# A causal attention block with a ternary feed-forward on one core: how the value products read and write their columns, and how the first score tile is formed

## The reference, cut to what matters

```python
# x: (2, 1024, 256) float32; 16 heads of 128
x = x + attention(layernorm(x), W_Q, W_K, W_V, W_O)
x = x + ffn(layernorm(x))                 # ternary weight, scale and shift, bias
...
q = einsum('bsd,hed->bhse', x, W_Q)       # k and v likewise
scores = where(causal, -1e9, einsum('bhse,bhme->bhsm', q, k) / sqrt(128))
z = einsum('bhsm,bhme->bhse', softmax(scores), v)
out = einsum('bhse,hde->bsd', z, W_O)
```

## Time and profile before

| | |
|---|---|
| time, median of 3 runs | 820.55 us (819.53 to 821.32) |
| the profiled execution | 819.02 us, of which the span of the instructions is 816.9 us |
| busy: PE, DVE, ACT, POOL | 808.9, 655.7, 558.7, 547.2 us |
| granted TensorE clock, mean | 1.000 |

### The profile page before, as it was taken

How to read it: one execution, slowest core, us unless ns; L and a number is a source line. 1 busy time by engine, 2 the same in 40 slices (tenths; PEclk the granted TensorE clock), 3 DMA queues, 4 the chain that set the end, 5 groups by cost and what they waited for, 6 DMA issues and landing times.

```text
span 816.9 us, 14674 instructions
## 1 busy us (share of the span) xinstructions
PE 808.9 (99%) x4878; PEld 726.5 (89%) x4878; DVE 655.7 (80%) x1438; ACT 558.7 (68%) x1031; POOL 547.2 (67%) x280
## 2 busy tenths in 40 slices
PE   8999999999999999999999999999999999999998
PEld 7988998888999888998888899888899888899887
DVE  7988787878777878778877878877878787878888
ACT  6877666667676666676766766666766766776684
POOL 6178765686666856768557785569675686585486
PEclk9999999999999999999999999999999999999999
DMA  6456656556556565566654676555766555555603
GB/s 187 95 140 144 171 136 142 117 135 166 138 134 151 134 153 123 139 146 149 161 122 112 152 177 143 127 119 126 175 140 141 130 130 141 128 138 137 150 6 105
DMA packets 57226, 111.50 MB, mean 136 GB/s; under 512 B 16960, under 2 KB 21184, under 8 KB 57152
## 3 DMA queue, kind: packets, MB, share of 16 engines
q1 hardware_dynamic: 57152, 110.56, 56.6%
HBM read 10.88 MB, written 2.10 MB: 16 GB/s over the span
## 4 chain that ended last, share of the span: by engine, by line
PE 95%; DVE 2%; SPq 1%; ACT 1%; DMA 0%; issue 0%; POOL 0%; POOLq 0%; ACTq 0%
PE ring L650 25%; PE scores L688 25%; PE ring L627 21%; PE ring L636 11%; PE ring L659 11%; SPq L445 1%; PE ring L668 1%; PE scores L750 1%; PE ring L591 1%; DMA pT<-turn 0%; DVE acc L861 0%; DVE turn L849 0%; PE ring L601 0%; DVE scores L841 0%; DVE stats L879 0%
## 5 line engine op out<-in xcount | busy, mean ns | idle before, releaser
L521 POOL TENSOR_TENSOR pT<-pT 128x1024 fp32r<-128x1024 f32 x186 | 444.4, 2407 | 256.9 <-ACT pT L786 256.3
L841 DVE CUSTOM_DVE_ANT_0 scores<-scores,mask 128x128 f32<-128x128 f32 (+7 forms) x256 | 194.3, 759 | 148.0 <-PE scores L688 146.3
L779 ACT ACTIVATE turn<-scores,negmax 128x128 f32<-128x128 f32 (+7 forms) x256 | 189.1, 739 | 145.8 <-DVE negmax L841 80.2
L688 PE MATMUL scores<-kT,qT 128*128 128x512 f32 (+3 forms) x1152 | 234.2, 342 | 0.1
L650 PE MATMUL ring<-pT,v 128*128 128x512 f32 x1116 | 217.2, 348 | 0.1
L650 PEld LDWEIGHTS ring<-pT,v 128*128 128x128 f32 x1116 | 187.6, 189 | 28.8 <-issue 0.4
L786 ACT ACTIVATE pT<-pT 128x1024 fp32r<-128x1024 f32 x186 | 195.4, 1057 | 17.0 <-DMA pT<-turn 16.4
L688 PEld LDWEIGHTS scores<-kT,qT 128*128 128x128 f32 x1152 | 186.6, 189 | 19.2 <-ACT turn L779 0.9
L849 DVE STREAM_TRANSPOSE turn<-turn 128x128 f32<-128x128 f32 (+1 forms) x248 | 187.3, 766 | 0.2 <-ACT turn L779 0.2
L659 PE MATMUL ring<-wo_s,zT 128*128 128x256 f32 x768 | 112.0, 282 | 0.2 <-DVE zT L912 0.2
L861 DVE SCALAR_TENSOR_TENSOR acc<-ring,inv,acc 128x256 f32<-128x256 f32 x256 | 109.7, 470 | 0.0
(11 more groups left out here) (79 smaller groups left out, 510.7 us busy)
## 6 DMA issues: line engine op xcount, KB each, us to landing
pT<-turn SPq DMA_DIRECT2D x496, 128.0 KB, 2.3
pT<-turn SPq DMA_DIRECT2D x496, 64.0 KB, 2.0
acc<-in_x SPq DMA_DIRECT2D x8, 256.0 KB, 5.5
wk_raw<-in_wk SPq DMA_DIRECT2D x8, 256.0 KB, 2.9
wq_raw<-in_wq SPq DMA_DIRECT2D x8, 256.0 KB, 3.7
wv_raw<-in_wv SPq DMA_DIRECT2D x8, 256.0 KB, 2.9
norm<-in_wo SPq DMA_DIRECT2D x8, 256.0 KB, 2.9
out<-acc SPq DMA_DIRECT2D x8, 256.0 KB, 2.5
```

Of the source, the lines that this page charges most:

```text
L521: pool.tensor_tensor(chunk(half, LO, c), f32(chunk(half, LO, c)), f32(chunk(half, HI, c)), ALU.subtract).then_inc(plo_ready, 1)
L688: mm = pe.matmul(scores[:, t % 2, first + c:first + c + n], qT[:, par, a, t * P:(t + 1) * P], kT[:, par, m, c:c + n], start=(i == 0), stop ...
L779: act.activation(turned, columns, ACT.Exp, bias=negmax[:, t % 2:t % 2 + 1], scale=-1.0, accum_out=rowsum[:, u % 2, t:t + 1]).then_inc(prob ...
L841: dve.tensor_tensor_reduce(out=tile, in0=tile, in1=mask[:, S - (t + 1) * P:S], scale=-1.0, scalar=FAR, op0=ALU.add, op1=ALU.min, accum_out ...
```

## The change

It does three things. (1) In `weighted_v` a product reads its probabilities block by block, as they are stored (a, then t and i), and writes them block by block into the bank, whose columns are now ordered (a, t, i); `split_target` puts them in token order when ScalarE and VectorE write `zT`. (2) Tile 0 of the scores is formed by two products: q HI with k HI and k LO side by side (256 columns), and q LO with k HI onto the second 128. (3) VectorE adds the two halves with a new `tensor_reduce` before the maximum of tile 0, with a new semaphore wait on its own result. The order of the steps in `weighted_v` is the same text before and after.

```diff
@@ score_columns @@
     def score_columns(t):
+        if t == 0:
+            return slice(2 * P, 3 * P)
         return slice(first_column(t), first_column(t) + (t + 1) * P)
@@ semaphores @@
         scores_ready = sem("scores_ready")
+        sum_ready = sem("sum_ready")
@@ split_target @@
-            first, n = (HALF * item[1], HALF) if kind == "pv" else GROUPS[item[1]]
+            if kind == "pv":
+                hi, lo = (zT[:, a, item[1] * BANK:(item[1] + 1) * BANK].rearrange("p (t a i) -> p a t i", a=A, i=Q)
+                          for a in (HI, LO))
+                return [(hi, lo, bank.rearrange("p (a t i) -> p a t i", a=A, i=Q), None)]
+            first, n = GROUPS[item[1]]
@@ weighted_v @@
                     lo, (a, m) = unseen(half, j), PASSES[i]
-                    seen = pT[half][:, m, :, j, lo * Q:P].rearrange("p a (t i) -> p t a i", i=Q)
-                    mm = pe.matmul(dst[:, lo * P:BANK], v[:, batch(u), a, j, hh * E:(hh + 1) * E], seen,
+                    mm = pe.matmul(dst.rearrange("p (a c) -> p a c", a=A)[:, :, lo * Q:P],
+                                   v[:, batch(u), a, j, hh * E:(hh + 1) * E], pT[half][:, m, :, j, lo * Q:P],
                                    start=(n == 0), stop=(n == len(steps) - 1))
@@ score_tile @@
                 width = (t + 1) * P
+                if t == 0:
+
+                    dst = scores[:, 0, 0:2 * P]
+                    pe.matmul(dst.rearrange("p (m c) -> p m c", m=2), qT[:, par, HI, 0:P], kT[:, par, :, 0:P],
+                              start=True, stop=False)
+                    pe.matmul(dst[:, P:2 * P], qT[:, par, LO, 0:P], kT[:, par, HI, 0:P],
+                              start=False, stop=True).then_inc(scores_ready, 1)
+                    return
@@ max_tile @@
                 tile = scores[:, t % 2, score_columns(t)]
+                if t == 0:
+                    dve.tensor_reduce(tile, scores[:, 0, 0:2 * P].rearrange("p (m c) -> p c m", m=2), AX_X,
+                                      ALU.add).then_inc(sum_ready, 1)
+                    dve.wait_ge(sum_ready, u + 1)
                 dve.tensor_tensor_reduce(out=tile, in0=tile, in1=mask[:, S - (t + 1) * P:S], scale=-1.0, scalar=FAR,
```

## The result

The changed kernel takes 816.65 us (median of 9 runs, 813.64 to 819.22), the kernel before beside it 819.83. The ratio is 0.9954 (95% interval 0.9939 to 0.9969), a gain of 3.8 us. The forecast was a gain of 6.6 us and 814.0 us; the time lies inside its range. Against the median of three runs that the prediction started from (820.55) the gain is 3.9 us. The sign was right, and the size of the forecast 2.7 to 2.8 us too large.

The account below looks back on a forecast made before the run. TensorE was taken to bound the kernel, busy 808.9 of 816.9 us. Tile 0 -3.4, reading order -3.7 and stalls +0.5 gave -6.6 us, from the median 820.55 to 814.0 us; range 811.0 to 818.6.

Parts of the forecast that it names:

- Part 1, tile 0: First score tile on TensorE: two weight loads, 0.34 becomes 0.23 us, 0.11 less in 32 units, -3.4 us (2.9 to 3.8).
- Part 2, the addition: VectorE's new reduction before max 0: 0.43 + 0.1 us more per unit, 16 us over the span, fitting its idle gap.
- the last rival: Reduction takes 0.87 us, tile 2 stalls some 0.2 us in half the units: 817 or 820.9 us; chance 0.09.
- the stalls: TensorE's waits at tile 2 on exp 0, tile 7 on exp 5 and the like: +0.5 us together (0 to 1.5).
- TensorE's saving does not use that up: Tile 7 waiting on exp 5 has 0.75 us to spare; TensorE's 0.23 us saved per unit leaves it enough.
- Part 3, the order of reading: Value products read in 4 runs: 5.0, 3.3, 1.7 ns less each, 0.12 us per unit, -3.7 us (0 to 4.6).
- more comes back: Rival: slow score tiles behind pv 0 are an after-effect of value products; 2.3 us more gained, 811.4 us; chance 0.09.
- A tick of 2.4 GHz per run: Value products' reads: each run of 32 columns costs about 0.41 ns, explaining 0.2333 against 0.2267 us at 512 columns.
- the order brings nothing: Rival: reading order of value products gains 0, as score tiles reading straight also take 0.232; 817.7 us; chance 0.24.
- Part 4, the splits: ScalarE and VectorE writing zT in runs of 32: no extra cost taken for either.
- The narrow one costs its load wherever it stands: Narrow value products, second, fourth and sixth in the job: wide plus narrow is 0.347 us, so moving them matters little.
- Writing in pieces: Rival: narrower value products writing four PSUM runs take two ticks per column, 50 us more, 863 us; chance 0.08.

Follow-up runs that it names:

- the order alone: Kernel before with only the value products' reading order and the split behind them changed, tile 0 as before: ratio 0.9967, gain 2.7 us.
- full change: The changed kernel with all three parts of the diff, against the kernel before: 816.65 us, ratio 0.9954; once more unaltered, 0.9951.
- the tile alone: Kernel before with only the first score tile changed (two products, the addition on VectorE), value products as before: ratio 0.9988, gain 1.0 us.

## Why the prediction was right or wrong

**What bounds the kernel.** Right for the steady unit, which got shorter by what TensorE's jobs did, 0.20 us. PE busy came to 804.5 us, not near 802, and the chain lies on TensorE for 89%, not 95%.

**Part 1, tile 0.** Expected -0.11 us per unit, measured -0.09 (24.35 to 24.25 with this part alone): -3.0 in place of -3.4. Tiles 0 and 1 lost 0.10 (0.69 to 0.59; tile 0 alone 0.28 to 0.18, where the prediction took 0.34 to 0.23), and the k products behind them got 0.01 longer.

**Part 2, the addition.** Right in its price and its cover. The rows of the changed kernel:

```profile
424.27 0.43 DVE L857 TENSOR_REDUCE scores<-scores 128x128 f32<-128x256 f32 x1 [1.20 <-PE scores L695]
424.73 0.30 DVE L860 CUSTOM_DVE_ANT_0 scores<-scores,mask 128x128 f32<-128x128 f32 x1
...
427.31 0.57 DVE L860 CUSTOM_DVE_ANT_0 scores<-scores,mask 128x384 f32<-128x384 f32 x1 [0.51 <-PE scores L703]
```

0.43 us, the next instruction 0.46 after its start, and an idle gap still ahead of max 2 (0.51 beside 0.79). The prediction had about 0.5 us for the two together. VectorE's busy time rose by 10 us and not by 16. Reading in steps of 128 columns was free: the upper bound of 0.87 was not needed. The run without it takes the same time, so the last rival (the addition as the wait) is out. The sign set for it (waits over 0.1 us at tile 2 in many units) would have misled: such waits came in four units, and without the addition too.

**The step that failed is the stalls: +0.5 us, bounds 0 to 1.5.** The waits were named (tile 2 on exp 0, tile 7 on exp 5, both behind a transfer) and sized by the kernel before's 0.9 us over the span. The steady gain was 6.2 us, 0.9 less than the two terms; 3.8 to 4.0 came through, so the stalls and what goes with them cost about 2.3 us, 1.8 more than the term and outside its bounds. In the profiled pair the wait grew by 4.2 - 0.9 = 3.3 us. The prediction read the slack of one clean unit (1.37 us) and held it against TensorE's gain per unit. It did not ask what happens to a unit in which the transfer is late by more than a microsecond, though the rows showed it: 41 waits of exp for a transfer, 64.7 us in all and up to 2.9. In that trace the late landings lay ahead of exp 4; in the changed kernel's, four lay ahead of exp 0, 1.1 to 2.0 us late, where the slack is about a microsecond (a landing 1.94 us late made TensorE wait 0.83 us). "TensorE's saving does not use that up" is true of clean units and beside the point in the others.

**Part 3, the order of reading.** The direction was right, and the size nearly: -0.11 us per unit in place of -0.12. But that is in part luck. The value products gave 0.08 (4.73 to 4.68 and 1.94 to 1.91 us), and the rest came from the jobs behind pv 0, which the sum had at nothing: with the order alone the k products there take 1.37 us in place of 1.39 and tiles 6 and 7 2.60 in place of 2.62. That is the rival "more comes back", true in part. (Its own time is 811.65 us by the forecast's terms, 813.95 - 2.3, and not 811.4; with the upper bound of part 3 it is 810.75.)

"A tick of 2.4 GHz per run" is not borne out as it stands. Wide products read in 16 runs take 0.2333. With 4 runs it asks for 0.2283; with nothing narrow ahead they take 3.40 / 15 = 0.2267, the same as q products read in one run, and writing in 16 runs costs nothing. Whether 16 runs cost by their number, or by an address pattern of one more dimension, no run tells apart. In the full change the ten wide products take 0.231, since after the narrow ones some are slower (224 to 236 ns, in a fixed sequence) and settle at 227; q products, which read straight, show a like sequence in both kernels (233, 236, 228, 233, 230 ns), so it does not need the new order of reading.

The rival "the order brings nothing" is out: the order alone brought 2.7 us (1.6 to 3.8). The rule of the Trainium skill (Advanced Engine Details and Errata, SBUF Cachelines) that two hits on each line of 16 bytes suffice for the full rate would have made part 3 nothing and the time 817.7 us. The runs disagree, by 0.2333 against 0.2267 us per product.

**Part 4, the splits.** Right: ScalarE's split of a pv bank took 594 ns in place of 596, VectorE's 685 in place of 686.

**The narrow products.** "The narrow one costs its load wherever it stands" holds for the unit nearly, and not for the job: with them last the job of 24 products got 0.11 us shorter and that of 12 0.05, the jobs behind took 0.13 back, and the unit gained 0.03.

**Writing in pieces.** Out, by 4.68 us for the job with 16 runs per product. The sentence of the Trainium skill on any non-contiguous pattern (Advanced Engine Details and Errata, PSUM Cachelines) does not hold for runs of 32 columns. Its condition that every two consecutive elements adjoin is met by these runs, and the trace agrees with it.

**Open.** The kernels with the new tile 0 meet a late landing ahead of exp 0 more often. There are 1 to 4 of them (23 in all) in seven profiles with tile 2 in its old place and the steps as before, with 2.4 to 5.3 us of waits; in three with the old tile 0 there are 0, 1 and 1, with 0.2 to 0.9 us. The packets are as many in both, and with the old tile 0 the late landings are there too, five or six in a profile, but ahead of exp 4. So what differs is at which place of the unit a packet comes, and why the new tile 0 moves that is not settled. It is not the addition, nor the count of instructions per unit. Nor is it the slack alone: from the start of the last issue of half 0 to tile 2 the median unit has 3.92 us before, 3.83 with the tile alone and 3.84 with the order alone, and the last of these waits only 0.6 us. Each profile is one execution, so part of the difference can be chance; the times (1.0 of 3.0 us through, against 2.7 of 3.3) say that not all of it is.

## What to carry to other kernels

Read the slack of the worst unit, not of a clean one: where an engine is in one long chain, what counts of a wait is how late its transfer comes in the bad cases. Look for that at the landing as well as at the issue: here the issue looked normal and the landing was 1 to 2 us late. A consumer of such a transfer wants its place in the order later by that much. A new instruction on an engine with a gap ahead of its next wait cost nothing here, though it added 10 us to that engine's busy time. Read operands in the order in which they lie (0.08 us of 6.67 per unit here); short products at the end of a job brought 0.03 us per unit, and writing the result in pieces of 32 columns cost nothing.

## What the runs showed of the hardware

- A packet of 16,384 bytes of instructions, about one in 20 us, coincides with late transfers. An issue on SyncE that meets one can take 0.8 to 2.2 us in place of 0.59 (31 of 32 long issues of the changed kernel overlap one; in the 14 traces 418 of 445 do, while 229 issues overlap one and stay under 0.75 us). A transfer of 64 KB in flight lands 2.6 to 4.1 us after its issue began in place of 2.0 (29 of 31 late ones in the 14 traces).
- Three score products of 128 columns cost 0.28 us, one of 256 and one of 128 0.18. The 0.10 us saved is near the distance of two weight loads at such products (0.113 us).
- A wide product of 512 columns repeats every 0.227 us at best, with reads in one run or in 4 runs of 128 columns, and every 0.233 with reads in 16 runs of 32. For some ten products after short ones it changes between 0.224 and 0.236 in the changed kernel.
- Writes of a product into PSUM in 16 runs of 32 columns cost the same as in one run (wide products) or four (narrower ones): a job of 24 products takes 4.68 us both ways.
- VectorE adds two blocks of 128 columns in PSUM, read in steps of 128 columns, in 0.43 us, as long as its maximum over 256 columns in a row.
